# Gated cross-attention on one core: VectorE adds four middle tiles of exponentials, and fold and sums become one set of narrow matmuls

## What is computed

```python
q = (layernorm(x) @ Wq + bq); k = (ctx @ Wk + bk); v = (ctx @ Wv + bv)     # 4 x 1024 x 512, 4 x 2048 x 512
attn = softmax(clip(q k^T * 32**-0.5, -1e4, 1e4))                          # per head: 1024 x 2048
x = x + tanh(g_xattn) * ((attn @ v) @ Wo + bo)
...
h = layernorm(layernorm(x)) with gamma, beta; w1, w2 = (codes - 128) * scales
x = x + tanh(g_ffn) * (layernorm(x) + 0.5 * (silu(h @ w1 + b1) @ w2 + b2))
```

## Time and profile before

| | us |
|---|---|
| median of 3 runs | 3039.09 (3038.51 to 3042.79) |
| profiled execution, whole | 3039.2 |
| its span in the profile | 3037.4 |
| PE busy | 2954.8 (97%) |
| DVE busy | 2159.4 (71%) |
| POOL busy | 1840.1 (61%) |
| ACT busy | 1632.3 (54%) |

### The profile page before, as it was taken

One profiled execution on the slowest core, in us unless ns is written; L12 is line 12 of the kernel. 1 busy time (PEld: TensorE's weight loads), 2 busy tenths in 40 slices (PEclk: granted clock), 3 DMA queues, 4 the chain that ended last, 5 costly groups with the idle time before them and its releaser, 6 DMA issues. The chain is left out here.

```text
span 3037.4 us, 51027 instructions
## 1 busy us (share of the span) xinstructions
PE 2954.8 (97%) x14950; PEld 1787.2 (59%) x14950; DVE 2159.4 (71%) x3162; ACT 1632.3 (54%) x2967; POOL 1840.1 (61%) x906
## 2 busy tenths in 40 slices
PE   8999979999999999999999999999989799999999
PEld 6888854444444444444444444444447577777777
DVE  5555557777777777777777777777768887777775
ACT  3222316666666666666666666666642444444443
POOL 4655538888888888888888888888863100000000
PEclk9999979999999999999999999999999899999999
DMA  5676761221221222222122122122249200000000
GB/s 198 226 236 217 237 216 43 64 62 43 63 63 46 60 63 53 52 63 59 46 63 62 43 63 63 48 57 63 50 130 318 96 29 28 29 29 25 17 14 28
DMA packets 142416, 255.25 MB, mean 84 GB/s; under 512 B 18970, under 2 KB 61042, under 8 KB 135156
## 3 DMA queue, kind: packets, MB, share of 16 engines
q1 hardware_dynamic: 142324, 254.13, 29.3%
HBM read 162.32 MB, written 91.23 MB: 83 GB/s over the span
## 5 line engine op out<-in xcount | busy, mean ns | idle before, releaser
L951 DVE TENSOR_REDUCE at_half_max<-ps 128x1 f32<-128x1024 f32 x1024 | 1216.6, 1219 | 461.3 <-PE ps L744 455.6
L744 PE MATMUL ps<-k_stack,q_stack 96*128 96x512 f32 x2048 | 707.5, 428 | 15.9 <-issue 12.1
L889 ACT ACTIVATE probT<-ps 128x512 f32<-128x512 f32 x1024 | 536.4, 603 | 230.1 <-PE ps L763 230.0
L763 PE MATMUL ps<-q_stack,k_stack 98*128 98x512 f32 x2048 | 657.2, 402 | 1.3 <-ACT probT L889 1.1
L889 ACT ACTIVATE at_probT<-ps 128x512 f32<-128x512 f32 x1024 | 536.4, 603 | 221.5 <-PE ps L763 221.5
L744 PEld LDWEIGHTS ps<-k_stack,q_stack 96*128 96x128 f32 x2048 | 350.2, 191 | 494.4 <-issue 326.5
L606 POOL TENSOR_TENSOR at_gp_sum<-at_gp_sum,at_probT 128x1024 f32<-128x1024 f32 x256 | 610.2, 2384 | 21.1
L606 POOL TENSOR_TENSOR at_gp_sum<-at_gp_sum,probT 128x1024 f32<-128x1024 f32 x256 | 609.9, 2383 | 21.4 <-ACT probT L889 0.4
L763 PEld LDWEIGHTS ps<-q_stack,k_stack 98*128 98x128 f32 x2048 | 386.2, 189 | 173.3 <-ACT probT L889 53.1
L1521 POOL TENSOR_TENSOR x_keep<-x_keep,b_half 128x512 f32<-128x512 f32 x32 | 42.7, 1334 | 529.1 <-DVE x_keep L1544 529.1
L1574 DVE SCALAR_TENSOR_TENSOR ff_acc<-ps,s_t,ff_acc 128x512 f32<-128x512 f32 x384 | 287.8, 749 | 20.0 <-DVE ff_acc L1574 0.5
(11 more groups left out here) (199 smaller groups left out, 3880.0 us busy)
## 6 DMA issues: line engine op xcount, KB each, us to landing
k_stack<-kT_hi SPq DMA_DIRECT2D x128, 256.0 KB, 4.9
kT_hi<-pi_out_hi SPq DMA_DIRECT2D x16, 1024.0 KB, 4.4
kT_lo<-pi_out_lo SPq DMA_DIRECT2D x16, 1024.0 KB, 6.7
v_heads<-pi_v_out SPq DMA_DIRECT2D x16, 1024.0 KB, 10.5
q_stack<-qT_hi SPq DMA_DIRECT2D x128, 128.0 KB, 3.4
k_stack<-kT_lo SPq DMA_DIRECT2D x64, 256.0 KB, 4.3
v_head<-v_heads SPq DMA_DIRECT2D x64, 256.0 KB, 5.1
pi_c_in<-in_ctx_dram SPq DMA_DIRECT2D x16, 768.0 KB, 10.1
```

The source lines that it names most:

```text
L744: mm = pe.matmul(ps[:, n, :], q_stack[buf][0:PARTS, rows], k_stack[buf][0:PARTS, BANK * n:BANK * (n + 1)], start=True, stop=True)
L763: pe.matmul(ps[:, key_bank(lane, kv), :], k_stack[buf][0:rows, P * kv:P * (kv + 1)], q_stack[buf][0:rows, q:q + BANK], start=True, stop=Tr ...
L889: act.activation(probT[lane % 2][:, kv, :], src, ACT.Exp).then_inc(exp_done, 1)
L951: dve.tensor_reduce(dst, src, AX_X, ALU.max).then_inc(max_done, 1)
```

## The change

Three things change.

1. DVE gets `add_rest`: for each unit but the last two it adds tiles 8 to 11 into `rest`, a 128 x 512 piece of the tile `clipped` that this path leaves idle, by a `tensor_reduce` over a view in which the four tiles are the innermost dimension. It does so in two halves of 256 columns: in step 3 and in step 0, both between the two `maxima`. So DVE reads 128 x 1024 elements for a half, each 2 KB behind the one before it, and writes 128 x 256.
2. POOL adds tiles 0 to 7 and 12 to 15 in place of 0 to 11: five additions as before. PE's `fold_values` and `last_sums` become one `fold_values` at the end of step 1: the fold, two matmuls for `gp_sum`, one for `rest`. For the last two units, PE still takes tiles 8 to 11 itself (seven matmuls, as before). ACT's `gather` moves from the middle of step 2 to its start.
3. The store of the last projected item moves behind the border: SP issues it in `attend`, once the first two score matmuls are done.

```diff
+        def store(sp, j):
...
+        H["store_last"] = lambda sp: store(sp, ITEMS - 1)
...
-                store(j - 3)
+                if j - 3 < ITEMS - 1:
+                    sp.wait_ge(hi_done, MT * (j - 2))
+                    sp.wait_ge(left, outs_by[j - 2])
+                    store(sp, j - 3)
...
-    TURN, KEYS, PV, SUMS, FOLD = 7, 8, (11, 12), 13, 14
+    TURN, KEYS, PV, FOLD, GATHER = 7, 8, (11, 12), 13, 14
+    REST = range(8, 12)
+    REST_PARTS = {PV[0]: slice(0, BANK // 2), PV[1]: slice(BANK // 2, BANK)}
...
+        rest = clipped[:, 0:BANK]
+        def by_pe(unit, clipping):
+            return clipping or isinstance(unit, int) and unit >= UNITS - 2
...
-                for i in range(1, GP_ADDS):
-                    pool.wait_ge(exp_done, KVT * unit + 2 * i + 4)
+                for i, first in enumerate((4, 6, 12, 14), 1):
+                    pool.wait_ge(exp_done, KVT * unit + first + 2)
                     pool.wait_ge(gp_added, GP_ADDS * unit + i)
                     pool.tensor_tensor(gp_sum[lane % 2][:, :, :], gp_sum[lane % 2][:, :, :],
-                                       pairs[:, 2 * i + 2:2 * i + 4, :], ALU.add).then_inc(gp_added, 1)
+                                       pairs[:, first:first + 2, :], ALU.add).then_inc(gp_added, 1)
...
             sp.wait_ge(score_done, 1)
+            H["store_last"](sp)
...
                 pe.wait_ge(partial_done, unit + 1)
-                pe.matmul(ps[0:D, 7, :], A["fold"][:, :], partial[:, :], start=True, stop=True)
-                for g in range(1, 4):
-                    mm = pe.matmul(ps[D * g:D * (g + 1), 7, :], ones[:, :], probT[lane % 2][:, KVT - 5 + g, :],
-                                   start=True, stop=False)
-                mm.then_inc(partial_read, 1)
-
-            def last_sums(base, slot):
-                unit, lane, r = unit_at(base, slot, FOLD)
-                if unit is None or r:
-                    return
                 pe.wait_ge(gp_added, GP_ADDS * (unit + 1))
-                for g, tile in ((1, probT[lane % 2][:, KVT - 1, :]), (2, gp_sum[lane % 2][:, 0, :]),
-                                (3, gp_sum[lane % 2][:, 1, :])):
-                    mm = pe.matmul(ps[D * g:D * (g + 1), 7, :], ones[:, :], tile, start=False, stop=True)
+                tiles = [gp_sum[lane % 2][:, i, :] for i in range(2)]
+                if by_pe(unit, clipping):
+                    tiles += [probT[lane % 2][:, kv, :] for kv in REST]
+                else:
+                    pe.wait_ge(rest_added, len(REST_PARTS) * (unit + 1))
+                    tiles.append(rest)
+                mm = pe.matmul(ps[0:D, 7, :], A["fold"][:, :], partial[:, :], start=True, stop=True)
+                for i, tile in enumerate(tiles):
+                    g = i % 3 + 1
+                    mm = pe.matmul(ps[D * g:D * (g + 1), 7, :], ones[:, :], tile, start=(i < 3), stop=(i + 3 >= len(tiles)))
                 mm.then_inc(fold_done, 1)
...
-                fold_values(base, slot)
-                last_sums(base, slot)
                 scores(base, slot, 2)
                 scores(base, slot, 3)
                 keys(base, slot, 2)
                 keys(base, slot, 3)
                 project_at(base, slot, (2, 3))
+                fold_values(base, slot)
...
             def step(base, slot):
+                gather(base, slot)
                 exps(base, slot, 0)
                 exps(base, slot, 1)
                 copy_partial(base, slot)
                 copy_maxima(base, slot)
-                gather(base, slot)
...
+            def add_rest(base, slot):
+                for lag, cols in REST_PARTS.items():
+                    unit, lane, r = unit_at(base, slot, lag)
+                    if unit is None or r or by_pe(unit, clipping):
+                        continue
+                    dve.wait_ge(exp_done, KVT * unit + REST.stop)
+                    need(dve, fold_done, unit)
+                    dve.tensor_reduce(rest[:, cols], probT[lane % 2][:, REST.start:REST.stop, cols].rearrange("p t n -> p n t"),
+                                      AX_X, ALU.add).then_inc(rest_added, 1)
...
                     maxima(slot, s, 0)
+                add_rest(base, slot)
...
             dve.wait_ge(max_done, 2 * STEPS)
+            dve.wait_ge(fold_done, UNITS - 2)
```

More of the change, by code:

```diff
@@ L184, in project_inputs @@
         block = ctx.enter_context(nc.Block())
+        def store(sp, j):
+            is_x, i = items[j]
+            chunks = (SQ if is_x else SK) // BANK
+            batch, chunk, par = i // chunks, i % chunks, j % 2
+            for part, o in ((0, out_hi), (1, out_lo)):
+                dst = (qT_d if is_x else kT_d)[part][C * batch:C * (batch + 1), BANK * chunk:BANK * (chunk + 1)]
+                sp.dma_start(dst.rearrange("(m p) n -> p m n", p=P), o[par][:, :, :].bitcast(F32)) \
+                    .then_inc(stored[par], 16)
+            if not is_x:
+                dst = v_d[HEADS * batch:HEADS * (batch + 1), :, TT * D * chunk:TT * D * (chunk + 1)]
+                sp.dma_start(dst.rearrange("h p n -> p h n"), v_out[par][:, :, :]).then_inc(stored[par], 16)
+        H["store_last"] = lambda sp: store(sp, ITEMS - 1)
         @block.gpsimd
@@ L216, in load_weight @@
                 sp.dma_start(w[n][:, :, :], src.rearrange("(k p) n -> p k n", p=P)).then_inc(w_in[n], 16)
[L218 to L230, removed]
             def load_heads():
@@ L493, in attend @@
     KVT = SK // P
-    TURN, KEYS, PV, SUMS, FOLD = 7, 8, (11, 12), 13, 14
-    TAIL = FOLD + 1 - QT
+    TURN, KEYS, PV, FOLD, GATHER = 7, 8, (11, 12), 13, 14
+    TAIL = GATHER + 1 - QT
     RING = 3
@@ L551, in attend @@
         partial_done = sem("partial_done")
-        partial_read = sem("partial_read")
+        rest_added = sem("rest_added")
         fold_done = sem("fold_done")
@@ L802, in fold_values @@
             def fold_values(base, slot):
-                unit, lane, r = unit_at(base, slot, SUMS)
+                unit, lane, r = unit_at(base, slot, FOLD)
                 if unit is None or r:
@@ L903, in copy_partial @@
                 act.wait_ge(pv_done, unit + 1)
-                need(act, partial_read, unit)
+                need(act, fold_done, unit)
                 act.copy(partial[:, :], ps[:, 7, :]).then_inc(partial_done, 1)
             def gather(base, slot):
-                unit, lane, r = unit_at(base, slot, FOLD)
+                unit, lane, r = unit_at(base, slot, GATHER)
                 if unit is None or r:
@@ L911, in gather @@
                 act.wait_ge(fold_done, unit + 1)
-                heads_before = (BODY * base + (slot - FOLD) // QT) // HALVES if isinstance(base, int) else \
-                    BUFS * base + (slot - FOLD) // PER_HEAD
+                heads_before = (BODY * base + (slot - GATHER) // QT) // HALVES if isinstance(base, int) else \
+                    BUFS * base + (slot - GATHER) // PER_HEAD
                 need(act, stored[lane % 2], 64 * heads_before)
@@ L1027, in step @@
                 shift(base, slot, 3)
-            run_steps(dve, step, STEPS, UNROLL, first=1, tail=TAIL if clipping else 0)
+            run_steps(dve, step, STEPS, UNROLL, first=1, tail=TAIL if clipping else PV[1] + 1 - 3 * QT)
         @block.vector
```

## The result

The changed kernel takes 3238.5 us (median, 3234.3 to 3240.9), the kernel before on the same chip 3040.4: a ratio of 1.066, 95% interval 1.064 to 1.067. The forecast was 2979, in a range of 2950 to 3125; 198 us were lost where 61 were to be won. The profiled execution took 3234.3 us, its span 3232.5, its mean granted clock 0.946 where before it was 0.986.

A forecast was written before the change was run, and what follows sets the result against it. PE bounds attention at 14.09 us a unit while DVE has slack. From 3039.2 us, minus 124.7 (narrow set), plus 65.7 (stall), minus 1 (border) gave 2979 us, range 2950 to 3125.

The forecast's parts named there:

- r: Time one new DVE reduction takes: 1.14 us assumed, 2.38 as the other end, break-even at 1.58.
- the rival of the hopping read: DVE reads hopping 2 KB at each element are slower: r 1.76, unit 14.43 us, 3080 us; chance 0.31.
- the clockwork: Step-by-step schedule of PE and DVE through one attention unit, giving 13.65 us against 14.09.
- the prediction's own rules: PE's stall in step 1 is r - 0.61; from r = 1.6 step 3 fills too, each further 0.1 costing 0.2.
- Narrow set: One set of PE narrow matmuls fewer in 126 units, 0.99 us each: 124.7 us saved.
- Stall at the second scores of step 1: PE waits there for DVE's second maxima of step 0: 0.53 us in 124 units, 65.7 us back.
- The fold set never waits on POOL: At the end of step 1, POOL's five additions are done at 7.8 us, the fold at 10.57: cover 2.8 us.
- POOL and DVE don't contend: Reductions run undisturbed beside POOL's additions; the rival of contention had r 2.2, 3189 us, chance 0.04.
- Step 3 hides its reduction: DVE's reduction between step 3's maxima is wholly hidden behind `values`, where DVE would have idled 1.60 us.
- The border: Moving the store lets PE start some 7 us sooner, given back waiting for `w_codes`: 1 us gain taken.
- The end of attention at nothing: POOL's last addition ends at 2268.9, still 1 us ahead of the last unit's fold: no cost.

The follow-up runs named there:

- the kernel with the filler: Changed kernel plus four narrow matmuls in PE's stall in the middle of step 1, results overwritten later by the fold set: 3128.8 us (1.0301).
- the kernel with neighbouring reads: Changed kernel, each reduction reading 1024 neighbouring elements of the same four tiles, so other sums than the reference's: 2991.9 us (0.9855).
- the kernel without reductions: Changed kernel with no DVE reduction; PE adds tile 8 instead, sums of tiles 9 to 11 left out: 2926.1 us (0.9635).
- one moved line: Changed kernel, fold set moved from the end of step 1 to just before its second scores: 3031.4 us (0.998).
- the two fastest kernels with all the sums: Changed kernel with fold set in mid step 1, 3031.4 us; with three two-region reductions and fold set in mid step 2, 3051.9 us.
- interleaved tiles, set moved: Changed kernel with ACT writing tiles 8 to 11 interleaved for neighbouring DVE reads, and fold set in the middle of step 1: 3341.0 us (1.1005).
- two-input additions: Changed kernel with fold set in mid step 1, each half summed by two two-tensor DVE additions instead of one reduction: 3445.5 us (1.1345).

## Why the prediction was wrong

**The step that failed is r, what one reduction occupies.** It was taken as 1.14 us "since all reductions in the trace, of either memory and of either shape, keep that rate"; it is 1.92. All those rows read neighbours, so they bore on another thing than the one in dispute: the order of reading. I gave the rival of the hopping read 0.31, and it was the case. The Trainium skill (Vector Engine (DVE) Microarchitecture Reference, Measured stream behaviour on trn2) has a number for such an order, though for an operation with two sources and hops of 4 KiB: the estimate from it was 1.84 us, and the trace has 1.92. Its remark that a one-source operation alternating between two regions keeps the full rate agrees with the run too (1.24 us, with 1.21 for neighbours).

**The rest of the clockwork held.** With r = 1.92 the prediction's own rules (stall r - 0.61, each 0.1 above 1.6 another 0.2 in all) give a stall of 1.31 and a unit of 14.75: 3038.2 + 124 x 0.66 = 3120. The changed kernel stalls 1.46 us on the average and its undisturbed units take 14.78; the kernel with the filler, where the clock is whole, takes 3128.8. With r near 1.14 it gave 2979 and units of 13.65, and the kernel with neighbouring reads took 2991.9 with units of 13.71.

**The second step that was missing is the clock.** Idle of PE was priced at its own length, and what the clock does behind it at nothing, without a word on it. No sum of the prediction could reach 3238 at the measured r of 1.92: without the clock it ends at 3120. The sum of the runs, from one kernel to the next: 3037 before; -111 for the narrow set; +66 for the reductions at full rate; +137 for their slow reading; +108 for the clock: 3237. (The first step has the border in it.) The last is nearly as large as all that the change could win. The range reached up to r = 1.95, so it held the measured r; its upper end of 3125 was still 113 us too low, and that is the clock.

Point by point:
- Narrow set, 0.99 us each and 124.7 in all: 111 measured, since the kernel without reductions has units of 13.2 us where 14.09 - 0.99 makes 13.1, and PE is busy 1692 of its 1700 us.
- Stall at the second scores of step 1, released by the second maxima of step 0: the place and the releaser right, 1.46 for 0.53 (167.4 us in 115 waits from 500 to 2300 us, one a unit). Nowhere else in the steady state: right.
- The fold set never waits on POOL (no such release among PE's waits), and POOL and DVE don't contend: right.
- Step 3 hides its reduction: right with 1.14; with 1.92 it no longer does, as stated.
- The border: first scores "near 423", first keys "no sooner than 450": 421.72 and 450.48, for 429.94 and 451.93 before. A gain of 1.5 us at that place, priced at 1; the run with the border alone shows nothing in the time. The codes were issued at 434.15 (before: 433.01) and landed 15.6 us later, at 449.8, just ahead of the keys: the place that the prediction named.
- The end of attention at nothing: nothing there shows in the difference; not tried by itself.

## What to carry to other kernels

A price taken from rows needs rows that are alike in what is in dispute, here the order in which one operand is read; where there are none, a measured number for that order weighs more than a pattern over rows of another order, as it did here. Price TensorE's idle not by its length alone: where a stall of over a microsecond is new in each round, look at the granted clock, and put work that is owed anyway into the stall: one moved line was worth 206 us here. And when work goes to another engine, ask for its slack in each half-step and not in the sum: the two fastest kernels with all the sums fill VectorE to 98 and 95%, and came out within 0.5% of the kernel before.

## What the runs showed of the hardware

- A VectorE reduction that takes one element from each of four regions 2 KB apart: 2.00 us for 1024 elements; from two such regions 1.24; neighbours 1.21. Three regions and other distances were not run.
- TensorE's clock: with one idle of 0.3 to 0.8 us a unit (the filler) it stayed at 1.00. In the changed kernel, with one of 1.05 to 1.76 a unit, it fell to 0.50 for some 3 us behind 67 of 114 (mean 0.93). The idles with a fall behind them were 1.31 to 1.76 us, those without 1.05 to 1.68, so the length of a single idle doesn't settle it. Two idles of 0.60 and 0.42 us within 2 us went with falls as well (interleaved tiles, set moved: mean 0.95), two of 0.24 and 0.42 did not (1.00). With idles up to 4.0 us (two-input additions) the mean was 0.87.
- ScalarE writing 512 results with a step of 16 bytes: some 1.15 us for 0.60 (estimated from the mean of all); TensorE's narrow matmuls whose moving operand has that step, half of 16: 2.85 us for 1.92.
- A two-input VectorE addition of 256 results beside a GpSimd addition: 2.5 us for 0.42.
